# The second feed-forward's weights prepared among the experts' tiles: a two-layer transformer kernel on one core

## The reference: what is computed

```python
x = x + attn0(ln(x))        # 16 heads of 16, LoRA on q, k, v, ALiBi, causal
x = x + experts(ln(x))      # 8 experts, each token to the one with the largest logit: silu(x G) * (x U) @ Down, width 512
x = x + attn1(ln(x))        # 16 heads of 64, rotary positions, bias, causal
x = x + fp4_ffn(ln(x))      # width 704, all operands quantized to FP4 in blocks of 16
```

```python
def fp4_quant_dequant(x):                    # along the last dim, blocks of 16
    scale = max(max(abs(block)) / 6, 1e-12)
    return nearest(block / scale, [0, .5, 1, 1.5, 2, 3, 4, 6] with sign) * scale
gate = fp4(x) @ fp4(w_gate).T;  up = fp4(x) @ fp4(w_up).T        # w_gate, w_up: 704 x 256
out  = fp4(silu(gate) * up) @ fp4(w_down).T                      # w_down: 256 x 704
```

## Time and profile before

| | us |
|---|---|
| median of 3 runs | 2246.32 (2244.27 to 2254.89) |
| profiled execution | 2245.09 |
| its span, first to last instruction | 2243.3 |
| its mean granted TensorE clock | 0.941 |
| PE, DVE, ACT, POOL busy | 1901.6, 1772.7, 1318.7, 1022.3 |

### The profile page before, as it was taken

How to read it: one execution, slowest core, us unless ns; L and a number is a source line. 1 busy time by engine, 2 the same in 40 slices (tenths; PEclk the granted TensorE clock), 3 DMA queues, 4 the chain that set the end, 5 groups by cost and what they waited for, 6 DMA issues and landing times. The chain is left out here.

```text
span 2243.3 us, 52217 instructions
## 1 busy us (share of the span) xinstructions
PE 1901.6 (85%) x18502; PEld 1352.5 (60%) x18503; DVE 1772.7 (79%) x3801; ACT 1318.7 (59%) x2559; POOL 1022.3 (46%) x1198
## 2 busy tenths in 40 slices
PE   6989899889834997487899999999999898459999
PEld 4666666666632665155566667676767676336665
DVE  8888888888781444688798898989898977679997
ACT  4666666666652444275677686768676768144443
POOL 5433454334032000689757575757676752132222
PEclk8999999999757999799899999999999999679999
DMA  7000000000052333013100000000000000100000
GB/s 249 2 2 2 1 2 2 2 1 2 31 174 77 89 90 90 7 34 51 29 20 22 17 22 16 23 15 23 18 21 18 20 18 25 39 0 16 16 19 24
DMA packets 73800, 74.54 MB, mean 33 GB/s; under 512 B 11152, under 2 KB 67808, under 8 KB 73584
## 3 DMA queue, kind: packets, MB, share of 16 engines
q1 hardware_dynamic: 66960, 62.58, 9.5%
q0 software_dynamic: 6416, 8.95, 1.9%
q10 hardware_dynamic: 208, 0.11, 0.0%
HBM read 36.22 MB, written 18.61 MB: 24 GB/s over the span
## 5 line engine op out<-in xcount | busy, mean ns | idle before, releaser
L376 PE MATMUL a_bank<-w_in_sb,xnT_sb 128*128 128x512 f16 x1152 | 287.1, 387 | 44.6 <-DVE yT_sb L608 23.9
L439 ACT ACTIVATE prob_sb<-a_bank,neg_max_sb 128x128 f32<-128x128 f32 (+3 forms) x512 | 257.3, 533 | 71.1 <-DVE neg_max_sb L543 59.8
L1240 DVE TENSOR_REDUCE neg_max_sb<-a_bank 128x1 f32<-128x128 f32 (+3 forms) x512 | 235.4, 484 | 76.8 <-PE a_bank L969 72.8
L543 DVE TENSOR_REDUCE neg_max_sb<-a_bank 128x1 f32<-128x128 f32 (+3 forms) x512 | 235.9, 481 | 63.6 <-PE a_bank L294 63.6
L1129 ACT ACTIVATE probT_sb<-a_bank 128x512 f32<-128x512 f32 (+1 forms) x384 | 198.7, 526 | 136.3 <-PE a_bank L992 131.3
L447 ACT ACTIVATE p_hi_sb<-a_bank 128x384 f16<-128x384 f32 (+1 forms) x384 | 202.2, 526 | 121.7 <-PE a_bank L303 120.0
L550 DVE TENSOR_TENSOR p_lo_sb<-a_bank,p_hi_sb 128x384 f16<-128x384 f32 (+1 forms) x384 | 227.2, 593 | 38.3 <-ACT p_hi_sb L447 37.7
L303 PE MATMUL a_bank<-ident_f_sb,prob_sb 128*128 128x128 f32 x1280 | 208.3, 278 | 4.4 <-DVE p_lo_sb L550 3.1
L731 POOL TENSOR_TENSOR rope_w_sb<-t_buf_sb,sin_sb 128x256 f32<-128x256 f32 x128 | 145.5, 1136 | 139.6 <-DVE t_buf_sb L591 131.4
L376 PEld LDWEIGHTS a_bank<-w_in_sb,xnT_sb 128*128 128x128 f16 x1152 | 101.6, 99 | 152.9 <-DVE yT_sb L608 30.6
L289 PE MATMUL a_bank<-stack_sb 128*128 128x128 f16 (+3 forms) x512 | 149.7, 305 | 37.3 <-ACT prob_sb L439 19.3
(11 more groups left out here) (274 smaller groups left out, 5581.5 us busy)
## 6 DMA issues: line engine op xcount, KB each, us to landing
stack_sb<-stack_sb SPq DMA_DIRECT2D x256, 64.0 KB
sorted_rows<-zeros_sb SPq DMA_DIRECT2D x1, 4992.0 KB, 22.4
x_in_sb<-sorted_rows SPq DMA_DIRECT2D x39, 128.0 KB, 2.2
sorted_results<-y_moe_sb SPq DMA_DIRECT2D x39, 128.0 KB, 1.7
x_sb_sb<-L_attn_x SPq DMA_DIRECT2D x8, 512.0 KB, 9.8
w_raw_sb<-L_ffn_gate_bank SPq DMA_DIRECT2D x8, 512.0 KB, 3.9
w_raw_sb<-L_ffn_up_bank SPq DMA_DIRECT2D x8, 512.0 KB, 4.8
w_raw_sb<-L_ffn_down_bank SPq DMA_DIRECT2D x8, 512.0 KB, 6.0
```

Of the source, the lines that this page charges most:

```text
L376: last = pe.matmul(out, xnT[:, x, c, j * P:(j + 1) * P], w["in"][:, w_, c, cols], start=k == 0, stop=k == len(terms) - 1)
L439: last = act.activation(prob[g][:, off:off + L], S[(3 * h + g) % 2][:, off:off + L], ACT.Exp, bias=neg_max[:, i:i + 1])
L543: last = dve.tensor_reduce(neg_max[:, i:i + 1], S[(3 * h + g) % 2][:, off:off + L], AX.X, ALU.max, negate=True)
L1240: last = dve.tensor_reduce(neg_max[:, h % 2, i:i + 1], S[(3 * h + g) % 2][:, off:off + L], AX.X, ALU.max, negate=True)
```

## The change

The first block of `fp4_ffn` loses all its work but the statistics. The work on the weights moves into the steps of `moe_experts`, one piece per step:
- **The loop is gone.** All steps -1 to 41 are written out on every engine.
- **DVE** runs one group of passes per step, between L2038 and L2043 of the old numbering: gate in steps 0 to 6, up in 10 to 16, down in 20 to 26. The two passes that POOL did are now DVE's. The low part of gate and up comes in steps 8 and 18. That is 23 steps with an addition.
- **ACT** takes the high part in steps 7 and 17, and copies a transposed piece into `stage` (two buffers) in the step behind its transposes, always ahead of the silu.
- **PE** transposes one piece (four f16 or two f32 transposes) into the free half of bank XT, in steps 9 to 14, 19 to 24 and 27 to 32 (18 pieces), between the gate and up products and the transposes of the rows.
- **SP** loads gate at step -1, up at step 9, down at step 19, into the same ring `w_raw`; stores every piece to DRAM one step behind ACT's copy; and loads the columns of `w_in1` in 6 parts of 512 columns in steps 33 to 38. The bias of attention 1 comes in one DMA (1536 KB, 12 KB for each partition) in step 3.
- **The second feed-forward** loads `w_gu` and `w_dn` from DRAM with four DMAs. PE waits for them at its first product with each.

```diff
-L1_PARTS = (SLOTS - 7) // 2
+L1_PARTS = 6
...
+        if part == 1:
+            rest = [(self.bias[:, :], d["L1_attn_b_in"].unsqueeze(0).to_broadcast([P, 3 * HEADS * DH1]))]
...
+    stage = sb("quantized_stage", [P, 2, 2 * C * P], F16)
+    raw, quot, magic = (flat[:, k * RAW:(k + 1) * RAW] for k in range(3))
+    BEGIN = (0, 10, 20)
+    ROUND, HIGH, LOW, UNITS = 7, 7, 8, (9, 9, 7)
+    IN_AT = BEGIN[2] + UNITS[2] + H1_TILES
...
     def run(eng, step):
-        for s in range(-1, HEAD):
+        for s in range(-1, SLOTS + 3):
             step(s, s % 2, s // 2)
-        with eng.Fori(0, (TAIL - HEAD) // 2) as i:
-            step(i * 2 + HEAD, 0, i + HEAD // 2)
-            step(i * 2 + HEAD + 1, 1, i + HEAD // 2)
-        for s in range(TAIL, SLOTS + 3):
-            step(s, s % 2, s // 2)
...
+            for s in range(-1, SLOTS + 3):
                 step(s, s % 2, s // 2)
-                if s >= 2:
+                if s == -1:
+                    load_matrix(0)
+                if 2 <= s < 6:
                     l1.load_rest(sp, d, s - 2)
+                m = part_of(s, LOW + 1, 1)
+                if m and m[0] < 2:
+                    sp.wait_ge(s_wl, m[0] + 1)
+                    load_matrix(m[0] + 1)
+                if unit_at(s - 2):
+                    store_unit(*unit_at(s - 2))
+                if IN_AT <= s < IN_AT + L1_PARTS:
+                    sp.wait_ge(s_wt, 3 * H1_TILES)
+                    l1.load_columns(sp, d, s - IN_AT)
...
+                if unit_at(s - 1):
+                    wait(pe, s_wT, unit_at(s - 1)[2] + 1)
+                if unit_at(s):
+                    m, i, u = unit_at(s)
+                    n = P if i < H1_TILES - 1 else H1_LAST
+                    wait(pe, s_xT, s + 1)
+                    if m < 2:
+                        wait(pe, s_wl, m + 1)
+                        for k in range(2 * C):
+                            a, c = divmod(k, C)
+                            last = pe.transpose(XT[:, :].bitcast(F16)[:, 2 * D + k * n:2 * D + (k + 1) * n],
+                                                w_part[0:n, a, i * D + c * P:i * D + (c + 1) * P], ident_h[0:n, 0:n])
...
+                m = part_of(s, HIGH, 1)
+                if m and m[0] < 2:
+                    wait(act, s_step, QUANTIZED[m[0]])
+                    wait(act, s_wt, m[0] * H1_TILES)
+                    act.activation(w_part[:, 0, :], raw, ACT.Copy).then_inc(s_wh, 1)
+                if unit_at(s - 1):
+                    m, i, u = unit_at(s - 1)
+                    wait(act, s_wt, u + 1)
+                    wait(act, s_put[u % 2], 16 * (u // 2))
...
+                if g == 0:
+                    wait(dve, s_pad, 1)
+                    wait(dve, s_raw, LOADED[m])
+                    group = ops[0:1]
+                elif g < 4:
+                    group = (ops[1:3], ops[3:4], ops[4:6])[g - 1]
+                elif g == 4:
+                    group = [lambda: dve.tensor_tensor(q, q, e, ALU.add)]
+                    if name != "down":
+                        group = [lambda: dve.tensor_scalar(sc, sc, W1_SCALE, None, ALU.mult)] + group
+                elif g == 5:
+                    group = [lambda: dve.tensor_tensor(q, q, e, ALU.subtract)]
+                else:
+                    group = [lambda: dve.tensor_tensor(blocks_of(src), blocks_of(q), per_block(sc), ALU.mult)]
...
+                m = part_of(s, LOW, 1)
+                if m and m[0] < 2:
+                    wait(dve, s_wh, m[0] + 1)
+                    dve.tensor_tensor(w_part[:, 1, :], raw, w_part[:, 0, :], ALU.subtract).then_inc(s_wl, 1)
...
             def _(sp):
-                for m in ("gate", "up"):
...
+                for a in range(2):
+                    sp.dma_start(w_gu[:, a, :, :], gu_store.rearrange("p (a c n) -> p a c n", a=2, c=C)[:, a, :, :]).then_inc(s_gu_in, 16)
+                full = (RT - 1) * D
+                sp.dma_start(w_dn[:, 0:RT - 1, :].rearrange("p k n -> p (k n)"), dn_store[:, 0:full]).then_inc(s_dn_in, 16)
+                sp.dma_start(w_dn[0:LAST, RT - 1, :], dn_store[0:LAST, full:]).then_inc(s_dn_in, 16)
...
                     if on(s):
                         wait(pe, s_xl, s + 1)
+                        if isinstance(s, int) and s == 0:
+                            wait(pe, s_gu_in, 32)
```

More of the change, by code:

```diff
@@ L46 @@
 FP4_BLOCK = 16
+H1_TILES = -(-H1 // P)
+H1_LAST = H1 - (H1_TILES - 1) * P
+H1_PIECES = [(a, min(a + 256, H1)) for a in range(0, H1, 256)]
 LAGS0 = (4, 6)
@@ L1953, in _ @@
+            for r in range(2):
+                sp.wait_ge(s_put[r], 16 * (3 * H1_TILES // 2))
             sp.wait_ge(s_out[0], 16 * ((SLOTS + 1) // 2))
@@ L2024, in _, with then, quantize @@
             run(act, step)
+        @block.gpsimd
+        def _(pool):
+            pool.memset(raw[H1_LAST:P, (H1_TILES - 1) * D:], 0.0).then_inc(s_pad, 1)
         @block.vector
         def _(dve):
+            steps = 0
+            def then(ins):
+                nonlocal steps
+                ins.then_inc(s_step, 1)
+                steps += 1
+            def quantize(m, g):
+                name, width = MATRICES[m]
+                nb = width // FP4_BLOCK
+                src, q, e, sc = raw[:, 0:width], quot[:, 0:width], magic[:, 0:width], scale[:, 0:nb]
+                ops = fp4_quotients(dve, src, sc, inv[:, 0:nb], q, e)
+                if g == 0:
[10 more added lines that the diff above has]
+                    group = [lambda: dve.tensor_tensor(q, q, e, ALU.subtract)]
+                else:
+                    group = [lambda: dve.tensor_tensor(blocks_of(src), blocks_of(q), per_block(sc), ALU.mult)]
+                for op in group:
+                    wait(dve, s_step, steps)
+                    then(op())
+                if g == ROUND - 1:
+                    assert steps == QUANTIZED[m]
             def step(s, r, half):
@@ L2129, in _ @@
+        s_gu_in, s_dn_in = sem("gate_up_weights_loaded"), sem("down_weights_loaded")
+        with nc.Block() as block:
+            layernorm_stats(block, stats, None, 0, *s_ln)
             @block.sync
             def _(sp):
-                for m in ("gate", "up"):
-                    src = d[f"L1_ffn_w_{m}"]
-                    full = (RT - 1) * P
-                    sp.dma_start(raw[m][:, 0:(RT - 1) * D].rearrange("p (i k) -> p i k", k=D),
-                                 src[0:full, :].rearrange("(i p) k -> p i k", p=P)).then_inc(s_raw[m], 16)
-                    sp.dma_start(raw[m][0:LAST, (RT - 1) * D:], src[full:H1, :]).then_inc(s_raw[m], 16)
@@ L2155, in _ @@
-                dve.wait_ge(s_pad, 1)
-                for n_m, (m, width) in enumerate(MATRICES):
-                    dve.wait_ge(s_raw[m], 16 if m == "down" else 32)
-                    if n_m >= 2:
-                        dve.wait_ge(s_q, 2 * (n_m - 1))
-                    nb = width // FP4_BLOCK
-                    q, e, sc = quot[:, n_m % 2, 0:width], magic[:, n_m % 2, 0:width], scale[:, n_m % 2, 0:nb]
-                    for f in fp4_quotients(dve, raw[m][:, :], sc, inv[:, 0:nb], q, e):
-                        step(f())
-                    if m != "down":
-                        step(dve.tensor_scalar(sc, sc, W1_SCALE, None, ALU.mult))
-                    dve.tensor_tensor(q, q, e, ALU.add).then_inc(s_near, 1)
-                    if n_m:
-                        low(n_m - 1)
@@ L2317, in step @@
                         wait(pe, s_hqT, t + 1)
+                        if isinstance(t, int) and t == 0:
+                            wait(pe, s_dn_in, 32)
                         wait(pe, s_res, t - 1)
```

192 lines of the change are left out of this document (77 added, 115 removed).

## The result

The changed kernel takes 2215.11 us (median of 4 runs, 2208.99 to 2221.21), the kernel before on the same chip 2245.30 us (4 runs). The ratio is 0.984, 95% interval 0.9813 to 0.9866: a gain of 1.3 to 1.9%. The forecast was 2205 us, the range 2199 to 2219. So the gain was forecast as 40 us and came out as 30; over all runs of this study (39 of before, mean 2249.7 us; 15 of the changed kernel, mean 2214.9) it is 34.8 us, give or take 3.4. These runs are of more than one chip; in the three sets in which both kernels ran side by side the means differ by 31.8, 33.4 and 36.3 us.

A forecast was written before the change was run, and what follows sets the result against it. TensorE bounds the experts' tiles; VectorE and GpSimd passes in turn bound the weights block. 2243.3 - 45.4 + 3.9 + 1.7 - 0.6 = 2202.9 us of span, 2204.7 with the 1.8 around it, forecast 2205; range 2199 to 2219.

The forecast's parts named there:

- Block of weights, -45.4 us: Last layer's start: token pipeline begins at about 1937.6 instead of 1983.04 us, the weight load costing nothing; -45.4 us.
- Pieces, +3.9 us: Experts' steps on TensorE: 18 transposed pieces at 0.22 us each hold back the down products; +3.9 us.
- VectorE's passes, 0: Experts' steps: passes of 1.76 us mostly fit VectorE's gap of 1.89 us, small lateness won back; cost 0.
- Rival 2: Experts: VectorE's turn, 4.53 of 4.57 us, becomes the step; 2214 us, or 2244 with passes at 3.61; chance 0.12.
- ScalarE, matrices and stores, 0: Experts: high part and piece copies fit ScalarE's 2.31 us; matrix loads and stores delay nothing; cost 0.
- The bias, +1.7 us: SP queue, ahead of tile 5's rows: 1,536 KB bias delays them, broadcast extra counted by pieces; +1.7 us, bound 11.6.
- Columns of w_in1, 0: SP queue, experts' late steps: 512 KB columns, last issued in step 38, have 10 us until ScalarE reads them; cost 0.
- The loop, -0.6 us: Experts' loop written out: recovers the 0.6 us by which 34 old steps exceeded 4.57 us each; -0.6 us.
- Rival 4: Experts' written-out steps: code runs short on DMA rings shared with weights and stores; 2253 us at 1.5 us per step; chance 0.02.
- Attention 1, 0: Stage after the experts, code unchanged: expected to keep the same length, no term in the sum.
- signs of being wrong: Steps 0 to 26 over 0.1 us longer on average, x_in wait 5 us or more, or last-layer first-product gap beyond 13.
- the bias by its bytes: SP queue, tile 5: broadcast's extra time goes with bytes, costing 11.6 instead of 1.7 us; 2215 us; chance 0.17.

The follow-up runs named there:

- e6: Changed kernel with SP's side transfers issued behind the next tile's row load, and each of the 18 pieces transposed twice on TensorE; 2216.54 us, ratio 0.9835.
- e8: Changed kernel with side transfers behind the row loads, plus one 1408-element VectorE maximum ahead of each of 21 groups of passes; 2229.21 us, ratio 0.9883.
- e1: Changed kernel with all SP side transfers of a step issued behind the next tile's row load instead of ahead; 2212.51 us, ratio 0.9846.
- e5: Changed kernel with only the bias of attention 1 moved, behind the row load of step 4; 2214.68 us, ratio 0.9813.
- e3: Kernel before with the experts' loop written out and nothing else changed; 2249.00 us, ratio 1.0005.
- e10: Same kernel as e1, unchanged, run again for the length of attention 1; 2217.28 us, ratio 0.9846.
- rows first: The kernel of e1 and e10: changed kernel with all SP side transfers behind the next tile's row load; 2212.51 and 2217.28 us.

## Why the prediction was right, and where it was off

- *Block of weights, -45.4 us.* Right: 49.37 - 3.81 = 45.56. The load cost nothing, as reasoned; `w_gu` landed 5 us early.
- *Pieces, +3.9 us.* Right in kind and nearly in size: 4.2 us. Sixteen turns are 4.79 and the last one of gate and of up 4.89. e6 shows that it is the transposes themselves.
- *VectorE's passes, 0.* Right, and safer than I thought: the turn is 4.26 us, not 4.53. Rival 2 was given its place by a sum of durations that overlap. By that turn VectorE becomes the step at a pass of some 2.1 us (1.76 + 0.3) in plain steps and 2.3 in steps with a piece. Its mechanism exists, since e8 makes it happen.
- *ScalarE, matrices and stores, 0.* Right: no wait for any of them.
- *The bias, +1.7 us.* This step was mis-sized. The wait itself came out at 1.09 to 1.32 us, with a landing after 6.9 to 7.1 us where 7.1 had been worked out, so the cost does go by pieces and not by bytes. What failed is the step from the wait to its cost: it took a wait of TensorE at its own length, where on this engine without slack the wait was followed by a restart pause and slower products, and in two of three profiles by a turn at a lower clock. 4.0, 3.8 and 2.2 us in all, by e1 and e5 all of it due to the place of that one DMA. Why the clock fell twice and held once behind nearly the same wait stays open.
- *Columns of w_in1, 0.* This step failed. I asked only when ScalarE needs the columns, and not what stands behind them on SP: rows of the next tile, with a microsecond of slack, behind 512 KB and an issue that now and then takes 1.5 us. 1.5, 0, 1.0 and 1.3 us in four profiles; the 1.0 came with issues of usual length (0.43 and 0.49 us) and rows only 0.11 us late. My own text had just priced the same thing for the bias.
- *The loop, -0.6 us.* Right within 0.3 us (e3): -5.4 us by a stall in every trip, -0.3 measured between the turns and nothing in the times. The Trainium skill (Runtime: NRT & Kernel Launch, Instruction fetch mechanics) speaks of branches whose target lies outside the fetched window, and the prediction took every trip for one. A trip here is 72 matmuls and as many weight loads on TensorE, and no run has a loop of which it is known that it leaves the window; the rule itself isn't tested. Rival 4 had the instructions on the same rings as the weights; the page of the changed kernel's profile shows them on queues of their own (q8 and q14, the weights on q1), and the turns of e1 and e10 leave no room for a shortage.
- *Attention 1, 0.* In the profiled execution +4.6 us. The same kernel varied by 12 us there, with the number of stretches that had less than the full clock. Part of the missing 10 us may be that chance: over all runs the gain is 34.8 us where block and turns account for 45.6 - 7.8 = 37.8 (7.8 by which the 35 turns of the three profiles are longer in the mean than the 160.6 before). The difference of 3.0 is no larger than its uncertainty of 3.4. With the rows first, mean 2214.2 us of 11 runs, the two accounts are 35.5 and 42.0, which is 6.5 us apart at an uncertainty of 4. Whether the change makes attention 1 some 4 us longer, through the granted clock, stays open; no run here isolates it.

Of its own signs of being wrong none is clearly there. Beyond the forecast wait of 1.7 us the steps up to 26 were longer than forecast by 2.5 us in sum, 0.09 us each, just under the 0.1 that it had set as a limit. That the time lay inside the range owes something to the width of the upper side, which was set for two other rivals (the bias by its bytes, VectorE's turn) and not for what was found. Two of its sums were rounded down: 18 x 0.22 is 3.96, and 2204.7 with the 1.2 of the median is 2205.9; neither matters at this spread.

The best order, rows first, is 3.4 to 5.5 us shorter in the experts' turns (169.66, 167.93 and 167.55 against 164.15), and that can't be told in the times: 2214.2 us mean of 11 runs against 2214.9 of 15, with runs of one kernel spread over 20 us.

## What to carry to other kernels

Work taken from a stage that one engine holds up, and put into the idle time of engines beside a full TensorE, cost one tenth of what it gave back with the rows first (4.2 of 45.6 us) and a sixth in the order that was built (7.8), and the first price could be read in advance from one row: what the moved work adds to TensorE itself. On a DMA queue ask of each new transfer not when its data is needed but who stands behind it, and issue what a full engine waits for first. Add up an engine's turn from start to start. Price late rows at a full TensorE not by their lateness alone: in this kernel 0.9 to 1.1 us came on top even of 0.1 us, and 2.6 to 2.7 where the clock fell.

## What the runs showed of the hardware that was not expected

- A wait for rows of 1.1 to 1.3 us in a stretch where TensorE had been busy without a gap was followed by a granted clock of 0.66 over the next 4 us in one profile, 0.71 in a second and 1.00 in a third. The same wait cost 4.0, 3.8 and 2.2 us. Five waits of 0.97 to 1.24 us for VectorE, one in each turn, left the clock at 1.00 (e8).
- Rows late by 0.11, 0.29, 0.53 and 1.09 us at a clock of 1.00 cost 1.0, 1.3, 1.5 and 2.2 us: about 1 us on top, however short the wait.
- GpSimd operations of 0.73 us took up to 2.19 beside VectorE's passes, and made single VectorE operations longer by 0.1 to 0.55 us.
- A 1,536 KB broadcast DMA with 12 KB pieces landed in 7.1 us, 216 KB per us, where a 128 KB broadcast took 3.0. Of 113 DMA issues on SP in the experts' stage of the same profile 106 took 0.3 to 0.8 us and seven 1.15 to 1.77.
- Three executions with the loop had the same two long turns (4.91 and 4.81, 4.74 and 4.99, 4.89 and 4.84 us) in the same place, turns 9 and 10, and none other above 4.60. The cause is open.
- Attention 1 took 1037.5 to 1050.5 us in fourteen profiles of the same code, on several chips, and the stage ahead of the experts 698.9 to 707.2. Effects under 10 us are settled here by turns, not by times.
